# Attention and mixture-of-experts layer on eight cores: transposes of P queued one iteration earlier, shared weights cast on their way in

## The reference

```
xn = layernorm(x);  q, k, v = split(xn @ W + b)            # W: 1024 x 3072
x  = x + softmax(causal(q @ k.T / 32)) @ v                 # one head, 8192 keys
xf = layernorm(x)
routed = sum over the top 2 of 8 experts of p_e * (silu(xf @ w1[e]) @ w2[e])
shared = sigmoid(xf @ gate_w) * (silu(xf @ G) * (xf @ U) @ down)
x  = x + routed + shared
```

## Time and profile before

| | |
|---|---|
| median of 3 runs | 2566.11 us (2560.77 to 2568.11) |
| profiled execution | 2559.16 us |
| its longest core (3) | span 2557.4 us |
| spans of the 8 cores | 2544.4 to 2557.4 us |
| granted TensorE clock, mean | 0.933 to 0.940 |
| TensorE busy | 2134.7 us, 83% |
| VectorE, ScalarE, GpSimd busy | 729.2, 706.5, 50.9 us |

### The profile page before, as it was taken

The page is one execution under the profiler, slowest core; times in us unless marked ns, Lnnn a source line. Parts: engine busy times, 40 slices in busy tenths (PEclk is TensorE's granted clock), DMA queues, the critical chain, the costliest instruction groups (busy, mean ns, idle before and its releaser), DMA issues.

```text
span 2557.3 us, 26315 instructions; the slowest of 8 cores (2544.4 to 2557.4 us)
## 1 busy us (share of the span) xinstructions
PE 2134.7 (83%) x9600; PEld 928.8 (36%) x9600; DVE 729.2 (29%) x945; ACT 706.5 (28%) x1256; POOL 50.9 (2%) x175
## 2 busy tenths in 40 slices
PE   0446999989899897979771566999999999999999
PEld 0112343334343333433320222444444444444444
DVE  3422432442433525243332111303122130211203
ACT  3213333332433525353524222020211102011120
POOL 0000000000000000000000000000000000000000
PEclk9777999999999999989895788999999999999999
DMA  7463321440564415342316100003211112211013
GB/s 157 93 89 83 81 50 34 87 85 9 117 97 83 103 27 100 67 113 56 95 35 127 50 24 10 1 1 60 39 34 33 34 34 50 50 33 34 1 33 132
DMA packets 205247, 156.01 MB, mean 61 GB/s; under 512 B 176192, under 2 KB 176320, under 8 KB 204992
## 3 DMA queue, kind: packets, MB, share of 16 engines
q1 hardware_dynamic: 192320, 108.17, 18.0%
q0 software_dynamic: 12800, 46.16, 10.7%
HBM read 149.08 MB, written 14.68 MB: 64 GB/s over the span
## 4 chain that ended last, share of the span: by engine, by line
PE 71%; DMA 8%; ACT 7%; DVE 4%; SPq 3%; issue 2%; ACTq 2%; DVEq 2%
PE pO L917 17%; PE sp L896 17%; PE pO L546 9%; PE pO L515 9%; PE pO L427 4%; DMA xb<-xkv 4%; PE sp L358 3%; PE sp L816 3%; PE sp L821 3%; DMA xb<-xq 2%; SPq L229 2%; PE pO L266 2%; PE pO L866 2%; ACTq L51 2%; DVEq L51 2%
## 5 line engine op out<-in xcount | busy, mean ns | idle before, releaser
L917 PE MATMUL pO<-w_sb,hb 128*128 128x512 bf16 x2048 | 443.3, 379 | 0.0
L896 PE MATMUL sp<-Q_sb,w 128*128 128x512 bf16 x2048 | 443.3, 379 | 0.0
L926 DVE SCALAR_TENSOR_TENSOR O<-pO,c_sb,O 128x1024 f32<-128x1024 f32 x128 | 164.4, 1284 | 719.7 <-PE pO L917 719.7
L904 ACT ACTIVATE hb<-sp 128x1024 bf16<-128x1024 f32 x128 | 131.1, 1024 | 753.0 <-PE sp L896 753.0
L427 PE MATMUL pO<-V_sb,PTd 128*128 128x512 bf16 x1088 | 262.2, 397 | 73.1 <-DMA PTd<-P 68.6
L358 PE MATMUL sp<-K_sb,Q_sb 128*128 128x512 bf16 x1088 | 253.9, 388 | 53.1 <-ACT P L400 41.9
L917 PEld LDWEIGHTS pO<-w_sb,hb 128*128 128x128 bf16 x2048 | 200.4, 98 | 241.6
L896 PEld LDWEIGHTS sp<-Q_sb,w 128*128 128x128 bf16 x2048 | 200.4, 98 | 241.6
L515 PE MATMUL pO<-xlnT,wkv_sb 128*128 128x512 bf16 x1024 | 227.0, 384 | 58.3 <-DMA xlnT<-xlnb 58.3
L546 PE MATMUL pO<-wkv_sb,xlnT 128*128 128x512 bf16 x1024 | 232.1, 380 | 0.0
L816 PE MATMUL sp<-Q_sb,wgu 128*128 128x512 bf16 x256 | 111.9, 437 | 103.4 <-DVE hb L835 80.0
(11 more groups left out here) (80 smaller groups left out, 1028.5 us busy)
## 6 DMA issues: line engine op xcount, KB each, us to landing
xb<-xkv SPq DMA_DIRECT2D x64, 512.0 KB, 4.6
xb<-xq SPq DMA_DIRECT2D x32, 512.0 KB, 4.8
w<-w1p POOLq DMA_DIRECT2D x8, 2048.0 KB, 12.8
w_sb<-w2p POOLq DMA_DIRECT2D x8, 2048.0 KB, 13.0
out<-O SPq DMA_DIRECT2D x16, 512.0 KB, 2.6
wkv_sb<-wkvh POOLq DMA_DIRECT2D x2, 2048.0 KB, 31.3
wgus<-wguh POOLq DMA_DIRECT2D x1, 4096.0 KB, 34.7
wgu<-wgus SPq DMA_DIRECT2D x16, 256.0 KB, 2.9
```

Source lines behind the costliest of these rows:

```text
L896: p.emit("tensor", lambda e, e_i=e_i, th=th, fc=fc, dc=dc, nbq=nbq, jj=jj: e.matmul(sp[jj][:, nbq * 512:nbq * 512 + 512], w1_sb[e_i % 2][: ...
L904: p.emit("scalar", lambda e, th=th, fc=fc, jj=jj: e.activation(out=hb[th][:, fc * 1024: fc * 1024 + 1024], in_=sp[jj][:], func=AF.Silu), i ...
L917: p.emit("tensor", lambda e, th=th, tc=tc, fc=fc, nbq=nbq: e.matmul(pO[tc % 2][:, nbq * 512:nbq * 512 + 512], hb[th][:, fc * 1024 + tc * 1 ...
L926: p.emit("vector", lambda e, tl=tl, tc=tc, e_i=e_i: e.scalar_tensor_tensor(out=O[tl][:], in0=pO[tc % 2][:], scalar=c_sb[:, tl * 8 + e_i: t ...
```

## The change

It has two parts. In the attention loop `emit_PdmaT` is called for the tile of the same iteration, directly after `emit_exp`, before the V projections and the popped items. The scratch casts go away: the shared weights are loaded by GpSimd straight from the float32 inputs with a cast on the way, in front of the first expert's weights in GpSimd's list; SyncE's waits ahead of them go too.

```diff
@@ attention loop
-            if pend:
-                pt_, ph, pr, psc, _ = pend[-1]
-                v_pte = emit_PdmaT(pt_, ph, pr, psc)
-                pend[-1] = (pt_, ph, pr, psc, v_pte)
             v_nmnew = emit_softmax(t, halves, masked, r, t_qk, sc_exp_parity[r % 2])
             sc_exp = emit_exp(t, halves, r, v_nmnew)
             sc_exp_parity[r % 2] = sc_exp
-            pend.append((t, halves, r, sc_exp, None))
+            v_pte = emit_PdmaT(t, halves, r, sc_exp)
+            pend.append((t, halves, r, sc_exp, v_pte))
...
-        pt_, ph, pr, psc, _ = pend[-1]
-        v_pte = emit_PdmaT(pt_, ph, pr, psc)
+        pt_, ph, pr, psc, v_pte = pend[-1]
...
-        if kb in (2, 4) and cast_q:
-            p.wait("gpsimd", T, T.n)
-            cast_q.pop(0)()
@@ feed-forward
-    p.wait("sync", T, t_attn)
-    p.wait("sync", SC, sc_attn)
-    for _s in range(3):
-        p.wait("sync", TRDs[_s], trd_all_xfT[_s])
-    p.wait("sync", PTR[0], ptr_last[0])
-    p.wait("sync", PTR[1], ptr_last[1])
-    p.wait("sync", CST, cst_all)
...
-        p.emit("sync", lambda e, fn=fn, li=li: e.dma_start(
-            out=wgu_sb[li][:, 0:1024], in_=wgus[:, fn * 2048:fn * 2048 + 1024]),
-            inc=GU[li], inc_n=16)
+        p.emit("gpsimd", lambda e, fn=fn, li=li: e.dma_start(
+            out=wgu_sb[li][:, 0:1024], in_=wguh[:, fn * 2048:fn * 2048 + 1024],
+            max_dma_last_dim=8192), inc=GU[li], inc_n=16)
...
-            p.wait("sync", T, t_wgu_free[fn % 2])
+            p.wait("gpsimd", T, t_wgu_free[fn % 2])
             load_wgu(fn)
         if fc == 0:
-            p.emit("sync", lambda e: e.dma_start(out=dw_sb[:], in_=dws), inc=DW, inc_n=16)
+            p.emit("gpsimd", lambda e: e.dma_start(out=dw_sb[:], in_=dwh, max_dma_last_dim=8192), inc=DW, inc_n=16)
```

More of the change, by code:

```diff
@@ L81, in build_program @@
     out = dram("out", [NT * 128, D], kind="ExternalOutput")
-    if stage == "full":
-        wgus = dram("wgus", [128, 8 * 2048], BF16, kind="ExternalOutput")
-        dws = dram("dws", [128, 8192], BF16, kind="ExternalOutput")
     es = ExitStack()
@@ L114, in build_program @@
     GU = [mk("GU0"), mk("GU1")]; GUB = [mk("GU0b"), mk("GU1b")]
-    W1S = [mk("W10"), mk("W11")]; W2S = mk("W2S"); CST = mk("CST")
+    W1S = [mk("W10"), mk("W11")]; W2S = mk("W2S")
     TRDs = [mk(f"TRD{i}") for i in range(3)]
@@ L331, in build_program @@
     lw_wv = WV.n
[L332 to L338, removed]
     p.wait("sync", T, t_phaseq)
@@ L784, in load_wgu @@
         li = fn % 2
-        p.emit("sync", lambda e, fn=fn, li=li: e.dma_start(
-            out=wgu_sb[li][:, 0:1024], in_=wgus[:, fn * 2048:fn * 2048 + 1024]),
-            inc=GU[li], inc_n=16)
-        p.emit("sync", lambda e, fn=fn, li=li: e.dma_start(
-            out=wgu_sb[li][:, 1024:2048], in_=wgus[:, fn * 2048 + 1024:fn * 2048 + 2048]),
-            inc=GUB[li], inc_n=16)
+        p.emit("gpsimd", lambda e, fn=fn, li=li: e.dma_start(
+            out=wgu_sb[li][:, 0:1024], in_=wguh[:, fn * 2048:fn * 2048 + 1024],
+            max_dma_last_dim=8192), inc=GU[li], inc_n=16)
+        p.emit("gpsimd", lambda e, fn=fn, li=li: e.dma_start(
+            out=wgu_sb[li][:, 1024:2048], in_=wguh[:, fn * 2048 + 1024:fn * 2048 + 2048],
+            max_dma_last_dim=8192), inc=GUB[li], inc_n=16)
         gu_ld[fn] = (GU[li].n, GUB[li].n)
```

## The result

The changed kernel takes 2753.1 us, median of ten runs, against 2565.4 us; the ratio is 1.0723, 95% interval 1.0703 to 1.0744. It is slower by 7.2%.

The account below looks back on a forecast made before the run. TensorE has most of the chain, but before the experts x loads set the pace of each block's first iterations. Terms 121 + 26 + 6 + 16 + 11 + 13 = 193 us gave 2760 us, 7.5% slower, range 2700 to 2815.

Parts of the forecast that it names:

- The closed loop: Attention blocks 0 to 4: x load waits for the exponential, the next exponential for that load; 14.0 us an iteration, loss 121 us.
- PT(1) to PT(5): Transposes of P of iterations 1 to 5; in blocks 0 to 4 expected 56 us apart in place of 32.
- The landing: Time from an x load's issue until it lands, taken as 4.7 us; 4.0 to 5.5 makes the loss 107 to 137.
- The residual loads: Iterations 6 and 7: loads leave later, behind P's transpose; 8.7 us a block in blocks 1 to 3, 26 us; block 4, 6 us.
- Blocks 5 and 6: Blocks popping four, and seven then six, items an iteration: K projection starts 16 us later in block 5, 11 in block 6.
- a cold start: TensorE's slower matmuls after a gap, 2.6 us each, expected before the K projections of blocks 4 to 6.
- TensorE's clock: Lower granted clock from waiting in the loops: 1.3 us each in blocks 0 to 3, 2.6 in blocks 4 to 6; 13 us.
- Block 7: No x tiles to load; one swapped pair costs SyncE 1.3 us with cover, so nothing was taken.
- The rest of the change: Removed scratch casts and shared weights through GpSimd's queue: loads hidden, 39 us of cover at the start; cost 0.
- Row loads that stay hidden: Rival: three buffers keep row loads hidden and only the earlier transpose of P counts; about 9 us faster, 2557 us; 4%.
- a delay once a block: Rival: the third buffer absorbs the rest, so delay comes once a block, not once an iteration; 74 us, 2640; 7%.
- A TensorE that becomes the loop: Rival: at 1.2 GHz throughout, TensorE also binds iterations 5 and 6; about 11 us more in each of five blocks, 2815; 8%.

Follow-up runs that it names:

- Experiments 2: Changed kernel with only the x loads of the coming items issued ahead of the transpose of P: 2551.0 us, ratio to before 0.9967.
- 4: Sums of a fresh x tile done one item later than its load: in the changed kernel 2569.2 and 2570.4 us, in the kernel before 2509.9 us.
- 3: Changed kernel with the x loads between the transpose of P and the row transpose, from iteration 1 on: 2717.3 and 2722.5 us.
- experiment 5: Changed kernel with only the residual loads issued ahead of the transpose of P: 2692.6 and 2696.0 us, ratio 1.0531.
- experiment 1: Kernel before with only the transposes of P moved: 2747.7 us; changed kernel with those transposes put back, only the weights' direct load left: ratio 0.9999.
- experiment 6: Changed kernel with x and residual loads ahead of P's transpose: 2504.4 us; the same with P's transposes back in their old place: 2496.9 us.

## Why the prediction was right, step by step

The forecast was 2760 us, measured 2753. The main mechanism and its size are borne out; the clock's term was four times too large, and the sum came out near also because smaller errors cancel, as told below.

**The closed loop** (2.56 + 4.85 + 6.62 = 14.0 us; 121 us). Shown. In the five blocks PT(1) to PT(5) took 55.7, 54.6, 56.5, 56.0 and 56.8 us, forecast 56.1. Against 159.2 us in the five blocks before, that is 120.5 us. Experiments 2 and 4 cut the loop at two different places, and either brings the total back to within 0.4% of the kernel before, with some gain in it that this kernel could have had too; 3 shortens the loop and the total follows.

That the sum of rows, 14.03 us, met the measured mean of 13.98 is in part luck. Over the 20 loops the three pieces were 2.69, 4.60 and 6.69 us in the mean. The median loop took 13.7: its load reached the sum after 4.44 us, where 4.85 was taken. Four loops took 14.7 to 15.6, two because the row transpose kept the load back by 1 us more, two because the load landed late (5.7 and 6.1 us), and lift the mean. The landing was the soft number. Over all loads of this line its median is 4.8, where the rows before gave 4.7; in the loops alone it is 4.3:

```profile
DMA to landing us min/median/max: 4.0/4.8/25.1
```

That is the view of line 243 after, all loads. By the Trainium skill (DMA: Bandwidth & Descriptors, Anatomy of one DMA) it would be an estimated 3.2 us; that fit is for DMAs issued by GpSimd, and these are issued by SyncE. The trace does not agree, and the measurement decides.

**The residual loads** (8.7 us a block, 26). From PT(5) to PT(8) blocks 1 to 3 took 8.6, 7.7 and 8.2 us longer; sum 24.6. Block 4 took 3.9 us more from PT(5) to PT(7), forecast 4.2, and 2.1 more from there to the K projection, forecast 1.7. By the traces this step holds; experiment 5 mixed it with an older wait.

**Blocks 5 and 6** (16 and 11 us, with a cold start 19.0 and 13.8). Measured 18.7 and 12.8. For block 6 the terms are right too: 11.6 us from the end of exp(1) to the K projection, forecast 11.2. For block 5 the agreement is luck. From PT(1) it took 19.5 us more, forecast 16.4, and no cold K projection stands in its step. The end of the chain shows the term that was short: between PT(4) and PT(5) the normalisation waited until a row transpose, issued behind PT(4), had landed, so 7.7 us where the forecast has 4.9. The last wait ahead of the K projection is for the rescale of O behind a residual load, as forecast. The chain of block 5 after:

```profile
1290.00 1.22 SPq L402
1291.26 3.23 DMA xlnT<-xlnb
...
1297.65 1.22 SPq L402
1298.92 4.04 DMA xb<-xq
1303.11 1.24 DVE O L473
...
1306.35 1.29 DVE O L436
...
1307.99 29.30 PE pO L505 x128
```

**TensorE's clock** (13 us). This is the term that was mis-sized. The granted clock did fall in the loops, as expected; a window of block 1's loops after (columns as in the earlier trace rows):

```profile
503.00:558.00 55.00, 36.47 (x129) 14.20 (x130) 18.84 (x26) 21.09 (x47) 1.86 (x9) 0.80 0.31 76
```

What it cost is read where no late load hides it. In block 0, which has no residual loads, PT(5) to PT(8) took 21.8 us against 20.0. Behind the last loop the granted clock was 0.60 (349 to 357 us), mostly the 1.2 GHz level, and the 16 matmuls there took 6.44 us, in the kernel before 3.61 (TensorE's timeline, after and before):

```profile
349.58 6.44 PE L348 MATMUL sp<-K_sb,Q_sb 128*128 128x512 bf16 x16 [3.90 <-ACT P L390]
...
326.95 3.61 PE L358 MATMUL sp<-K_sb,Q_sb 128*128 128x512 bf16 x16 [1.74 <-ACT P L400]
```

That is 1.8 us for block 0, where 1.3 was taken. In blocks 1 to 3 the slow matmuls (6.36 us in block 1) run while VectorE waits for a residual load, and PT(5) to PT(6) is 0.5 us longer at most. Ahead of the K projections at the end of blocks 4 to 6 three cold starts, 7.8 us, were taken. One shows: the 128 matmuls from 1307.99 took 29.3 us, where the others behind the first K projection, before and after, took 27.8, so 1.5 us. Products with V ahead of them are slow too (5.0, 5.4 and 5.8 us for 16 matmuls, where 3.6 is usual), but they do not stand in the chain; the K projection waits for VectorE's rescale. So the clock cost 3.3 us, not 13.

**How the sum came out.** The measured terms are 120.5 for the loops, 24.6 and 6.1 for the residual loads, 19.5 and 11.6 for blocks 5 and 6, 3.3 for the clock and 1.6 for block 7: 187 us. Block 7 was taken as nothing. There the residual load leaves 2.65 us behind the last transpose of P instead of 1.31; the rest of it was not followed. From the start of the K projection to PT(1) blocks 0 to 5 were 3.7 us shorter in all, which no term had and nothing here explains. That leaves the 183.3 of the spans. So the forecast's 193 is 10 too long, as much as the clock's error; the short term of block 5 and block 7 are offset by the gain ahead of the loops. The lower end of the range, 2700, is not what the named terms give, 2733.

**The rest of the change** (0). Shown by experiment 1, to 0.1%.

**The other rivals.** Row loads that stay hidden, and a delay once a block: both are excluded by the 14 us spacing, which repeats in all 20 loops, 13.4 to 15.6 us each. A TensorE that becomes the loop would have cost about 11 us a block in iterations 5 and 6; the clock did fall to 0.80, but in blocks 0 to 3 the loops and PT(5) to PT(8) account for the steps to within 2.4 us. The forecast's remark that something is gained in blocks 5 and 6 because P no longer waits for the last row transposes was in the sums. Expected by itself, as 9 us in experiment 6, it did not appear.

## What to carry to other kernels

In a queue that runs strictly in order, look at what stands behind the instruction that you move forward, not only at what stands ahead of it. A load placed behind a transpose inherits its wait. Then follow the load's consumer in its own engine's order; if it stands ahead of what releases the load, the two close a loop, and its length is the sum of durations that the old trace already has. The cheap cures are to issue loads ahead of anything that waits for this iteration, and to let a fresh tile's first use come one item later.

## What the runs showed of the hardware

Over 55 us of loops TensorE's granted clock was 0.80 in the mean, partly at 1.2 and partly at 2.4 GHz, and cost nothing there: a loop of 14 us held 6.9 us of work at full speed. A low granted clock in a window is no price by itself. It is paid only where matmuls are what is waited for, here 1.8 us behind the loops of block 0 and 1.5 us in one K projection.

A load of 512 KB that SyncE issued 1.26 us behind a transpose and directly ahead of another took 5.0 us until its sum began, in the median of 20; issued behind both it took 4.4.
